# The order of TensorE's work in an attention stage, and who writes the rows of ones

## The chip, the core and the metric

The kernel runs on one core of a Trainium2 chip. The metric is the device time of one execution in microseconds (us), measured from outside; the profile's span is the part of it between the first and the last recorded instruction. Times below that come from the profile belong to one profiled execution. A core has five engines, each with its own queue of instructions: TensorE (PE, with its weight loads PEld), VectorE (DVE), ScalarE (ACT), GpSimd (POOL) and SyncE (SP), which here issues nearly all transfers (DMAs). An instruction that waits for a semaphore holds up all that is queued behind it on its engine.

## The reference, cut to what matters

The program is two transformer layers. The change touches the first attention alone: 2 sequences of 512 tokens, 32 query heads of width 8, of which each four share one of 8 key and value heads.

```python
q = bitlinear(x, wq).reshape(B, S, N_KV, G, HEAD_DIM)      # B 2, S 512, N_KV 8, G 4, HEAD_DIM 8
k = bitlinear(x, wk).reshape(B, S, N_KV, HEAD_DIM)
v = bitlinear(x, wv).reshape(B, S, N_KV, HEAD_DIM)
scores = jnp.einsum('bskgd,btkd->bkgst', q, k) * sm_scale
scores = jnp.where(causal, scores, -jnp.inf)
probs = jax.nn.softmax(scores, axis=-1)
out = jnp.einsum('bkgst,btkd->bskgd', probs, v)
```

Behind it come a gated feed-forward layer, a recurrent mixing layer with a scan over time, and a mixture of 32 experts with a shared one, each between layer norms with residuals. None of their instructions changes.

## The kernel before

The order of every engine's queue is written out by hand. The attention works on 16 groups (`NG`): one sequence and one key head with its four query heads, 512 by 512 scores a head. The scores of a group are computed twice. First as **rows** (queries on the partitions): VectorE takes from them the negated maximum of each query, `negm`. Then as **columns** (keys on the partitions): the maxima, brought back as extra rows of the query operand, are subtracted inside the product, so that ScalarE's exponential can write `probs` at once, keys first, as the product with the values wants them. The keys' operand `k_all` has rows of ones (partitions 32 to 63 and 96 to 127) which carry these extra rows through the product.

The loop is a software pipeline over slots n = 0 to 19 (`slots`). In slot n TensorE does, of group n, six units of score rows (`score_rows`, list `ROWS`); of group n-2, five pairs of score columns (`score_cols`, list `COLS`); of group n-3, the product with the values for four key tiles (`weighted`, called "value products" here); and in odd slots `out_rows`, which turns the finished outputs of two groups into rows. Before, the order within a slot is a loop over u = 0 to 5: rows u, then (u = 0, odd slot) `out_rows`, columns u, and value products by the table `PV_AT`.

What sets the order around it:
- Row units take turns on two pairs of PSUM banks: unit u waits until VectorE has reduced unit u-2 (`s1_read`). Columns take turns on three banks, two for a pair, so the next pair waits for ScalarE's first exponential of the pair before (`st_exp`).
- VectorE in slot n reduces the six row units. After unit 1 (`MT_AT`) it transposes the split maxima of group n-1 (`m_cols`), and in odd slots after unit 0 it divides (`DIV_AT`).
- ScalarE in slot n does the ten exponentials of group n-2, and in even slots after the last (`OC_AT` = 9) the copy `o_cols` for which the `out_rows` of the next slot waits.
- GpSimd zeroes the future keys in `probs` (four instructions a group, semaphore `hidden`) and between them splits the maxima of group n into two parts.
- SyncE in slot n loads the queries of group n+1 (`load_q`, six DMAs), then waits for `m_cols` of group n-1, writes it to DRAM in four DMAs (L545), waits for them, and loads it into the query operand in two (L549). The columns of group n-1 wait for these. In slot 1 it first loads the keys of the second sequence (`load_k(1)`, four DMAs) and their rows of ones (`ones_rows(1)`, two DMAs).

After the attention ScalarE and TensorE go on with the first output product and the feed-forward layer; what is behind it starts when the attention's last groups are done.

## Time and profile before

| | us |
|---|---|
| median of 3 runs (lowest, highest) | 647.87 (647.41, 648.37) |
| the profiled execution | 645.54 |
| its span | 643.8 |
| PE, DVE, ACT, POOL busy | 457.6, 385.6, 248.9, 231.4 |
| score rows of group 0 start on TensorE | 53.52 |
| first score columns start | 81.49 |
| one odd and one even slot in the steady part | 9.17 and 8.45 |

TensorE is busy for 71% of the span, but the mean hides stages with different limits: the profile's second section cuts the span in 40 slices of 16.1 us each, and the attention is slices 4 to 14. A busy TensorE is not one at full speed either; the row PEclk of that section gives the granted clock in tenths. The chain of waits is the view to read for what sets the end; the rows that are used stand below.

### The profile page before, as it was taken

What the parts mean: (1) busy time and instruction counts of PE and PEld (TensorE: products, weight loads), DVE (VectorE), ACT (ScalarE), POOL (GpSimd) and SP (SyncE); (2) the same over time, 40 slices, a digit from 0 to 9 for tenths busy, and PEclk for the clock granted to TensorE, in tenths of its full rate; (3) what the DMA queues carried; (4) which work ended last, traced back from release to release, by engine and by line L of the source; (5) the groups of instructions that cost most, each with busy time, mean ns of one, the idle gap of its engine ahead of it and who ended that gap; (6) DMA issues with size and microseconds to landing.
All of it is one profiled execution on the core that took longest, in us unless ns stands there. A gap on an engine that the chain in (4) does not pass through costs nothing.

```text
span 643.8 us, 9925 instructions
## 1 busy us (share of the span) xinstructions
PE 457.6 (71%) x3183; PEld 336.2 (52%) x3183; DVE 385.6 (60%) x940; ACT 248.9 (39%) x503; POOL 231.4 (36%) x310
## 2 busy tenths in 40 slices
PE   0365398888987869698954345596777999999660
PEld 0253254454444448577743334494665777877440
DVE  6833457777776256745497848863723555655344
ACT  1141056666668543225802450523312344433202
POOL 6911024333364631403102211165170455555500
PEclk9995559999999889897997566997897999999965
DMA  9177911111150039600000005984022344543061
GB/s 225 29 151 174 120 40 41 36 35 31 40 171 7 2 116 338 211 1 1 0 2 25 24 24 122 251 248 129 18 110 62 114 132 127 143 124 99 20 260 65
DMA packets 60146, 62.26 MB, mean 97 GB/s; under 512 B 10420, under 2 KB 51005, under 8 KB 60096
## 3 DMA queue, kind: packets, MB, share of 16 engines
q1 hardware_dynamic: 54928, 52.89, 32.4%
q0 software_dynamic: 5168, 8.74, 4.1%
q8 instruction: 27, 0.44, 0.3%
q14 instruction: 23, 0.19, 0.1%
HBM read 37.67 MB, written 25.75 MB: 99 GB/s over the span
## 4 chain that ended last, share of the span: by engine, by line
PE 49%; DVE 24%; issue 9%; ACT 6%; DMA 6%; POOL 2%; SPq 2%; another core or an unknown queue 1%; POOLq 0%; DVEq 0%; ACTq 0%
PE ps L2045 8%; PE ps L1789 5%; PE ps L2064 4%; PE ps L1839 4%; PE ps L1747 4%; PE ps L1768 4%; PE ps L1827 3%; PE ps L1828 3%; PE ps L1829 3%; PE ps L2035 3%; DVE xn L836 2%; DVE st L904 2%; DVE negm L1003 2%; DVE gain L1106 2%; ACT probs L1491 2%
## 5 line engine op out<-in xcount | busy, mean ns | idle before, releaser
L1491 ACT ACTIVATE probs<-ps 128x512 f32<-128x512 f32 x160 | 86.9, 595 | 66.6 <-PE ps L1768 64.8
L1000 DVE TENSOR_REDUCE negm<-ps 128x2 f32<-128x1024 f32 (+1 forms) x64 | 68.9, 1090 | 43.0 <-PE ps L1757 42.2
L813 POOL DMA_INDIRECT y_slots_scratch<-yblk,ids x63 | 62.0, 984 | 64.1 <-issue 26.4
L1747 PE MATMUL ps<-k_all,q_ring 64*128 64x512 f32 (+3 forms) x256 | 52.4, 416 | 22.6 <-DMA q_ring<-q_ring 10.8
L656 POOL TENSOR_TENSOR rstd<-ve,halfneg 128x4 f32<-128x4 f32 x16 | 16.6, 1035 | 128.6 <-DVE ve L935 80.6
L2045 PE MATMUL ps<-wgu,xcol 128*128 x252 | 58.1, 354 | 4.0 <-issue 1.5
L1768 PE MATMUL ps<-q_ring,k_all 64*128 64x512 f32 (+3 forms) x256 | 41.7, 382 | 19.1 <-DMA q_ring<-max_parts_scratch 9.9
L1747 PEld LDWEIGHTS ps<-k_all,q_ring 64*128 64x128 f32 x256 | 27.6, 207 | 48.5 <-issue 28.0
L1789 PE MATMUL ps<-probs,v_all 128*32 128x128 f32 (+3 forms) x512 | 47.0, 467 | 4.8 <-POOL probs L702 4.6
L2045 PEld LDWEIGHTS ps<-wgu,xcol 128*128 128x128 f32 x252 | 40.3, 193 | 12.6 <-issue 10.1
L1529 ACT CAST h_hi<-hf 128x512 fp32r<-128x512 f32 x28 | 17.4, 620 | 64.2 <-DVE hf L1058 55.6
L788 POOL DMA_INDIRECT x_sorted_scratch<-rows,dest x32 | 31.5, 984 | 25.9 <-DVE dest L1284 16.7
L1058 DVE TENSOR_TENSOR hf<-sg,ps 128x512 f32<-128x512 f32 x28 | 19.2, 685 | 35.9 <-ACT sg L1523 23.6
L702 POOL TENSOR_SCALAR_AFFINE_SELECT probs<-probs 128x512 f32<-128x512 f32 x64 | 39.8, 634 | 0.0
L2064 PE MATMUL ps<-wd,hcol 96*128 x126 | 38.7, 388 | 0.9 <-ACT yblk L1676 0.6
L1003 DVE TENSOR_REDUCE negm<-ps 128x4 f32<-128x1024 f32 (+1 forms) x32 | 29.3, 954 | 16.7 <-PE ps L1757 16.6
L1378 DVE TENSOR_TENSOR hb<-gb,ps 128x96 f32<-128x96 f32 x63 | 16.0, 253 | 35.3 <-ACT gb L1668 25.5
L1768 PEld LDWEIGHTS ps<-q_ring,k_all 64*128 64x128 f32 x256 | 22.0, 198 | 26.2 <-ACT probs L1491 14.1
L694 POOL TENSOR_TENSOR waited<-zero 128x1 f32<-128x1 f32 x48 | 9.2, 192 | 73.6 <-ACT probs L1491 73.5
L1361 DVE COPY xcol<-ps 128x256 f32<-128x256 f32 x63 | 26.6, 422 | 13.4 <-PE ps L2035 13.2
L1668 ACT ACTIVATE gb<-ps 128x96 f32<-128x96 f32 x63 | 15.8, 251 | 46.9 <-PE ps L2045 38.9
L1676 ACT COPY yblk<-ps 128x256 f32<-128x256 f32 x63 | 23.4, 372 | 24.0 <-PE ps L2064 22.4
(290 smaller groups left out, 1284.9 us busy)
## 6 DMA issues: line engine op xcount, KB each, us to landing
x_sorted_scratch<-pad SPq DMA_DIRECT2D x7, 1206.0 KB, 13.5
xblk<-x_sorted_scratch SPq DMA_DIRECT2D x63, 134.0 KB
wgu<-in_moe_w SPq DMA_DIRECT2D x4, 1536.0 KB
q_ring<-q_parts_scratch SPq DMA_DIRECT2D x64, 64.0 KB
ycomb<-y_slots_scratch SPq DMA_DIRECT2D x8, 512.0 KB, 6.9
wd<-in_moe_w SPq DMA_DIRECT2D x1, 3072.0 KB, 18.6
sraw<-in_moe_w SPq DMA_DIRECT2D x6, 384.0 KB, 3.3
k_all<-ones SPq DMA_DIRECT2D x4, 512.0 KB, 11.3
```

The costliest lines, as they stand in the source:

```text
L702: pool.affine_select(out=tiles, in_=tiles, compare_op=ALU.is_ge, fill=0.0, base=0, pattern=[[0, GQ], [1, P]], channel_multiplier=-1).then_ ...
L788: pool.indirect_dma_start(out=x_sorted, out_offset=bass.IndirectOffsetOnAxis(ap=dest[:, u, j:j + 1], axis=0), in_=rows[:, u, :], in_offset ...
L813: pool.indirect_dma_start(out=y_slots, out_offset=bass.IndirectOffsetOnAxis(ap=ids[:, i:i + 1], axis=0), in_=yblk[:, i % YR, :], in_offset ...
L1000: dve.tensor_reduce(negm[:, par, :, hp, qt], pair_of, AX.X, ALU.max, negate=True).then_inc(s1_read, 1)
L1003: dve.tensor_reduce(negm[:, par, :, :, qt], pair_of.rearrange("p a (h t) -> p a h t", h=nh), AX.X, ALU.max, negate=True).then_inc(s1_read, 1)
L1361: dve.tensor_copy(xcol[:, i % 2, :], ps[:, i % 2, 0:D]).then_inc(bt_copied, 1)
L1491: act.activation(probs[:, par, u, :], ps[:, col_unit(g, u), :], ACT.Exp)\
L1747: pe.matmul(ps[:, u % 2 * 2 + rg, end - w:end], q_ring[lane(rg, 64), g % QRING, h0 + h, qt * P:(qt + 1) * P], k_all[lane(rg, 64), g * T:g ...
L1768: mm = pe.matmul(ps[:, col_unit(g, 2 * p + rg), c:c + w], k_all[lane(rg, 64), g * T + kt * P:g * T + (kt + 1) * P], q_ring[lane(rg, 64), g ...
L1789: mm = pe.matmul(ps[32 * h:32 * h + 32, 7, kt * P:T], v_all[:, (g * TPB + kt) * 32:(g * TPB + kt + 1) * 32], probs[:, g % 2, un, c:c + T - ...
L2045: mm = pe.matmul(ps[:, 2 + i % 2, 0:2 * F].rearrange("p (w f) -> p w f", w=2), xcol[:, i % 2, k * P:(k + 1) * P], wgu[:, k, :, bass.ds(e * ...
L2064: pe.matmul(ps[:, 4 + i % 2, 0:D], hcol[0:F, i % 2, :], wd[0:F, bass.ds(e, 1), :].rearrange("p o d -> p (o d)"), start=True, stop=True).th ...
```

## The change

TensorE's order within a slot becomes a table, `ORDER`. `out_rows` stands at the head of an odd slot, then come the first pair of columns, and the last thing in a slot are the first two row units of the next group ("next"). The value products wait for as many of GpSimd's four instructions as they need (1, 2, 4, 4) and no longer all four. VectorE transposes the maxima after row unit 0. The product with the Hadamard matrix in slot 0 (L1873) moves from behind row unit 3 to behind row unit 4. The rows of ones are written by ScalarE, in four copies of 32 partitions by 4096 elements: two at its very start, one in slot 1 behind its last copy of slot 0, one in slot 2 behind the exponentials of group 0. SyncE's four DMAs for them go, and `load_k(1)` moves from slot 1 to the end of slot 3.

```diff
@@ -257,6 +257,7 @@
         s_x = [sem("x0_loaded"), sem("x1_loaded")]
         s_const = sem("consts_loaded")
         s_constb = sem("bf16_consts_loaded")
+        k_ones = sem("key_ones_rows_ready")
         s_w = sem("attn_weights_loaded")
         s_dve = sem("vector_order")
         s_pool = sem("pool_order")
@@ -396,8 +397,12 @@
         RU, CU, QD = len(ROWS), len(COLS), 96
         SLOTS = NG + 4
         FIRST, PAIRS = 4, 4
-        MT_AT, DIV_AT, OT_AT, OC_AT = 1, 0, 0, 9
-        PV_AT = {1: [0], 2: [1], 3: [2, 3]}
+        MT_AT, DIV_AT, OC_AT = 0, 0, 9
+
+
+        ORDER = (("cols", 0), ("rows", 2), ("values", 0), ("cols", 1), ("rows", 3), ("cols", 2),
+                 ("rows", 4), ("values", 1), ("rows", 5), ("cols", 3), ("values", 2),
+                 ("values", 3), ("next", 0), ("cols", 4), ("next", 1))
 
         def slots(body):
 
@@ -509,17 +514,6 @@
                         q_ring[64 * rg + MAX_AT + 2:64 * rg + MAX_AT + 4, g % QRING, :, :]
                         .bitcast(F32)).then_inc(q_in[g % 2], 16)
 
-            def ones_rows(b):
-
-                for rg in range(2):
-                    sp.dma_start(
-                        k_all[64 * rg + KP:64 * rg + 64, b * NKV * T:(b + 1) * NKV * T]
-                        .bitcast(F32).rearrange("r (n c) -> r n c", c=P),
-                        ones[0:64 - KP, :].unsqueeze(1).to_broadcast((64 - KP, NKV * T // P, P)))\
-                        .then_inc(k_in[b], 16)
-
-            sp.wait_ge(s_ready, 1)
-            ones_rows(0)
             spill(0)
             load_k(0)
             sp.wait_ge(q_spilled, 32)
@@ -530,9 +524,6 @@
             def slot(n, par, pair):
                 if n == 0:
                     spill(1)
-                if n == 1:
-                    load_k(1)
-                    ones_rows(1)
                 if n == FIRST - 1:
                     sp.wait_ge(q_spilled, 32 * B)
                 if 3 <= n + 1 < NG:
@@ -550,6 +541,8 @@
                             q_ring[64 * rg + MAX_AT:64 * rg + MAX_AT + 2, g % QRING, :, :]
                             .bitcast(F32), m_dram[g, rg].rearrange("(i hp) t -> i hp t", hp=2))\
                             .then_inc(m_in[g % 2], 16)
+                if n == 3:
+                    load_k(1)
 
 
                 after = n - (FIRST + 2 * PAIRS)
@@ -1428,6 +1421,16 @@
 
         @block.scalar
         def _(act):
+            def ones_rows(b, rg):
+
+                act.copy(k_all[64 * rg + KP:64 * rg + 64, b * NKV * T:(b + 1) * NKV * T]
+                         .rearrange("r (n c) -> r n c", c=P),
+                         ones[64 * rg + KP:64 * rg + 64, :].unsqueeze(1)
+                         .to_broadcast((64 - KP, NKV * T // P, P))).then_inc(k_ones, 1)
+
+            act.wait_ge(s_ready, 1)
+            ones_rows(0, 0)
+            ones_rows(0, 1)
             act.wait_ge(s_w, 64)
             for n in range(4):
                 cols = DC * (64 if n in (1, 2) else D)
@@ -1505,6 +1508,8 @@
                             1.0 / 32).then_inc(w2_hi_done, 1)
                     act.wait_ge(w2_hi_done, 1)
                     act.copy(w2hi[:, :, :], w2a[:, :, :]).then_inc(w2_hi_done, 1)
+                if n in (1, 2):
+                    ones_rows(1, n - 1)
                 if n in (NG - 2, NG - 1):
 
                     raw, hi = ((w1raw, w1hi), (w3raw, w3hi))[n - NG + 2]
@@ -1737,6 +1742,13 @@
             pe.wait_ge(k_split, B)
             pe.wait_ge(q_split, DC * B)
 
+            def rows_begin(g):
+
+                pe.wait_ge(q_in[g % 2], (g // 2 + 1) * QD)
+                if g % NKV == 0:
+                    pe.wait_ge(k_in[g // NKV], 64)
+                    pe.wait_ge(k_ones, 2 * (g // NKV + 1))
+
             def score_rows(g, u):
                 qt, h0, nh = ROWS[u]
                 need(pe, s1_read, RU * g + u - 1)
@@ -1783,7 +1795,7 @@
 
                 if kt == 0:
                     need(pe, att_ready, g // 2 * 2)
-                    pe.wait_ge(hidden, 4 * (g + 1))
+                pe.wait_ge(hidden, 4 * g + (1, 2, 4, 4)[kt])
                 for h in range(GQ):
                     un, c = WHERE[kt, h]
                     mm = pe.matmul(ps[32 * h:32 * h + 32, 7, kt * P:T],
@@ -1848,23 +1860,23 @@
                     pe.wait_ge(rows_ready, TPB)
                     transposes(1, 0, rows_tile(0))
                 if n == 0:
-                    pe.wait_ge(q_in[0], QD)
-                    pe.wait_ge(k_in[0], 96)
-                if has(n, 0) and n > 0:
-                    pe.wait_ge(q_in[par], pair * QD + QD)
-                if n == NKV:
-                    pe.wait_ge(k_in[1], 96)
-                for u in range(RU):
-                    if has(n, 0):
+                    rows_begin(0)
+                    score_rows(0, 0)
+                    score_rows(0, 1)
+                if has(n, 4) and n % 2:
+                    out_rows(n - 4)
+                for what, u in ORDER:
+                    if what == "rows" and has(n, 0):
                         score_rows(n, u)
-                    if u == OT_AT and has(n, 4) and n % 2:
-                        out_rows(n - 4)
-                    if has(n, 2) and u < CU:
+                    if what == "next" and has(n + 1, 0):
+                        if u == 0:
+                            rows_begin(n + 1)
+                        score_rows(n + 1, u)
+                    if what == "cols" and has(n, 2):
                         score_cols(n - 2, u)
-                    if has(n, 3) and u in PV_AT:
-                        for kt in PV_AT[u]:
-                            weighted(n - 3, kt)
-                    if n == 0 and u == 3:
+                    if what == "values" and has(n, 3):
+                        weighted(n - 3, u)
+                    if n == 0 and (what, u) == ("rows", 4):
 
                         pe.wait_ge(butterfly, 3)
                         pe.wait_ge(w2_split, 1)
@@ -1875,12 +1887,12 @@
                                     half[:, 2 * c:2 * c + 2, :].rearrange("p c d -> p (c d)"),
                                     start=(j == 0), stop=(j == 1))
                             mm.then_inc(w2_mm, 1)
-                    if n == NG and u == 2:
+                    if n == NG and (what, u) == ("values", 1):
 
                         pe.wait_ge(att_ready, NKV)
                         pe.wait_ge(s1_read, RU * NG)
                         transposes(0, 0, att_tile(0))
-                    if n == NG + 1 and u == 2:
+                    if n == NG + 1 and (what, u) == ("values", 1):
                         out_product(0)
 
             def mlp_up(u):
```

On TensorE, at the boundary between an even and an odd slot, this stands before (128x256 x4 are the last pair of columns, 128x128 x2 the last row unit, 128x512 x2 from `k_all` and `q_ring` the first row unit of the next group, `ident,o_cols` the turn `out_rows`, 128x512 x2 from `q_ring` and `k_all` the first pair of columns; the rows from `hide_cols` and `hide_swap` between them belong to the row units):

```order
L1768 MATMUL ps<-q_ring,k_all 128x256 x4
...
L1747 MATMUL ps<-k_all,q_ring 128x128 x2
...
L1747 MATMUL ps<-k_all,q_ring 128x512 x2
...
L1778 MATMUL ps<-ident,o_cols 128x128 x4
L1768 MATMUL ps<-q_ring,k_all 128x512 x2
```

And this at the same boundary after the change:

```order
L1780 MATMUL ps<-q_ring,k_all 128x128 x2
L1801 MATMUL ps<-probs,v_all 32x256 x4
L1801 MATMUL ps<-probs,v_all 32x128 x4
L1759 MATMUL ps<-k_all,q_ring 128x512 x2
...
L1780 MATMUL ps<-q_ring,k_all 128x256 x4
L1759 MATMUL ps<-k_all,q_ring 128x512 x2
...
L1790 MATMUL ps<-ident,o_cols 128x128 x4
L1780 MATMUL ps<-q_ring,k_all 128x512 x2
L1759 MATMUL ps<-k_all,q_ring 128x384 x2
```

Between the last pair of columns and `out_rows` there were two row units; now there is one.

On SyncE this stands before from the spill of the second sequence on (`k_parts_scratch`, `q_parts_scratch`) to the maxima of group 0:

```order
L477 DMA q_parts_scratch<-qparts_102 128x2x512
L485 DMA k_all<-k_parts_scratch 16x8x512 [waits k_parts_in_dram]
L485 DMA k_all<-k_parts_scratch 16x8x512 x3
L515 DMA k_all<-ones 32x32x128 x2
L545 DMA max_parts_scratch<-m_cols 32x32 [waits max_rows_ready]
L545 DMA max_parts_scratch<-m_cols 32x32 x3
L549 DMA q_ring<-max_parts_scratch 2x1024 [waits max_rows_even_in_dram]
```

And this after the change; the load of the keys stands 30 DMAs further on, behind the maxima of group 2:

```order
L482 DMA q_parts_scratch<-qparts_102 128x2x512
L536 DMA max_parts_scratch<-m_cols 32x32 [waits max_rows_ready]
L536 DMA max_parts_scratch<-m_cols 32x32 x3
L540 DMA q_ring<-max_parts_scratch 2x1024 [waits max_rows_even_in_dram]
L540 DMA q_ring<-max_parts_scratch 2x1024
```

Six DMAs in front of the first maxima are gone.

On ScalarE this is the start of the attention after the change; before, the two rows of `k_all` were not there:

```order
L1506 ACTIVATE w2a<-ps 128x2048 [waits w2_hadamard_done]
L1510 CAST w2hi<-w2a 128x2048 [waits w2_hi_ready]
L1426 CAST k_all<-ones 32x4096
L1494 ACTIVATE probs<-ps 128x512 [waits score_cols_full] x10
L1426 CAST k_all<-ones 32x4096
L1494 ACTIVATE probs<-ps 128x512 [waits score_cols_full] x10
```

The second of them stands between the exponentials of group 0 and those of group 1.

## Rows read from the trace of the kernel before

**Rows 1.** The page: the granted clock by slice of 16.1 us.
```profile
PEclk9995559999999889897997566997897999999965
```
**Rows 2.** The chain of waits in order of time: start us, us, what.
```profile
67.35 5.62 SPq L545
...
79.78 1.66 DMA q_ring<-max_parts_scratch
81.49 0.81 PE ps L1768 x2
```
**Rows 3.** SyncE's queue by time, 42 to 110 us: start, us, what.
```profile
61.73 2.54 SPq L485 DMA_DIRECT2D k_all<-k_parts_scratch  x4
64.31 1.33 SPq L515 DMA_DIRECT2D k_all<-ones  x2
...
102.47 1.80 SPq L545 DMA_DIRECT2D max_parts_scratch<-m_cols  x4
105.32 0.52 SPq L549 DMA_DIRECT2D q_ring<-max_parts_scratch  x2
```
**Rows 4.** DMA issues, 60 to 200 us: KB each, median us to landing.
```profile
k_all<-k_parts_scratch SPq DMA_DIRECT2D x4, 256.0 KB, 7.9
k_all<-ones SPq DMA_DIRECT2D x2, 512.0 KB, 12.8
...
max_parts_scratch<-m_cols SPq DMA_DIRECT2D x56, 4.0 KB, 1.4
```
**Rows 5.** VectorE by time, around slots 0 to 2.
```profile
62.83 1.82 DVE L1003 TENSOR_REDUCE negm<-ps 128x4 f32<-128x1024 f32 x2 [4.01 <-PE ps L1757]
...
69.58 1.82 DVE L1003 TENSOR_REDUCE negm<-ps 128x4 f32<-128x1024 f32 x2 [0.45 <-PE ps L1757]
```
**Rows 6.** ScalarE by time, start of the program and slots 0 to 3.
```profile
10.62 1.55 ACT L1434 ACTIVATE wsg<-wraw 128x512 fp32r<-128x512 f32 x4 [8.55 <-DMA wraw<-in_wo]
...
63.48 1.90 ACT L1507 CAST w2hi<-w2a 128x2048 fp32r<-128x2048 f32 x1
82.33 1.09 ACT L1491 ACTIVATE probs<-ps 128x512 f32<-128x512 f32 x2 [16.95 <-PE ps L1768]
```
**Rows 7.** Windows: stretch, length, busy of PE, PEld, DVE, ACT, POOL, then granted clock.
```profile
66.00:68.00 2.00, 1.48 (x12) 0.82 (x12) 2.00 (x4) 0.00 (x0) 0.00 (x0) 0.58 1.13 130
82.00:92.00 10.00, 9.49 (x74) 6.13 (x70) 6.86 (x8) 6.51 (x12) 3.31 (x9) 0.50 0.18 47
94.00:96.00 2.00, 2.00 (x26) 1.05 (x28) 0.96 (x1) 1.08 (x2) 0.33 (x1) 1.00 0.06 10
143.33:152.50 9.17, 8.06 (x100) 4.51 (x101) 6.96 (x11) 5.90 (x12) 3.30 (x9) 1.00 0.13 36
152.50:160.95 8.45, 7.35 (x96) 4.10 (x97) 6.22 (x8) 5.43 (x12) 3.30 (x9) 1.00 0.14 36
```
**Rows 8.** TensorE by time in the steady part: slot from 152.5 us, head of the next.
```profile
154.17 0.50 PE L1768 MATMUL ps<-q_ring,k_all 64*128 64x512 f32 x2 [0.41 <-ACT probs L1491]
...
155.59 0.45 PE L1747 MATMUL ps<-k_all,q_ring 64*128 64x384 f32 x2
...
159.37 0.49 PE L1768 MATMUL ps<-q_ring,k_all 64*128 64x256 f32 x4
...
160.95 0.51 PE L1747 MATMUL ps<-k_all,q_ring 64*128 64x512 f32 x2 [0.69 <-DVE negm L1003]
...
161.51 0.66 PE L1778 MATMUL ps<-ident,o_cols 128*128 128x128 f32 x4
162.10 0.51 PE L1768 MATMUL ps<-q_ring,k_all 64*128 64x512 f32 x2
```
**Rows 9.** ScalarE by time behind the last pair of columns of that slot.
```profile
159.90 1.09 ACT L1491 ACTIVATE probs<-ps 128x512 f32<-128x512 f32 x2 [0.73 <-PE ps L1768]
160.87 0.59 ACT L1499 COPY o_cols<-ps 128x512 f32<-128x512 f32 x1
```
**Rows 10.** VectorE by time: the division behind that `out_rows`.
```profile
163.19 0.49 DVE L1028 TENSOR_TENSOR att<-ps,rsum 128x128 f32<-128x128 f32 x2
```

## The prediction, on record before the run

> **What bounds the kernel now.** I read the clock row of the page first, then the chain of waits in order of time, then each engine's own timeline in the stretch that the change touches. The clock row [rows 1] is to be read as stages: slices 4 to 6 (48 to 96 us) stand at 5, half speed, the rest of the attention at 9 or full. So the attention has two parts, and the change means something else in each.
>
> The head, 53.5 to 94 us. The chain [rows 2] runs through transfers: the write of group 0's maxima to DRAM is issued at 67.35, one of its four issues takes 5.62 us, and only at 81.49 do the first score columns start. In SyncE's queue [rows 3] the reader is to see what stands in front: the keys of the second sequence at 61.73 and their rows of ones at 64.31. These are 4 x 256 KB and 2 x 512 KB, 2 MB, and take 7.9 and 12.8 us to land, where the maxima (4 KB each) take 1.4 us in the median [rows 4]. Later the same six DMAs of a group need 105.32 - 102.47 = 2.85 us from the first issue to the load back [rows 3]; the load itself lands in about 1.7 us [rows 2]. In the head it was 81.49 - 67.35 = 14.1 us in place of some 4.5.
>
> The steady part, 94 to 206 us. A pair of slots takes 9.17 + 8.45 = 17.62 us, at full clock, TensorE busy 8.06 and 7.35 of it [rows 7]. Its timeline shows two waits in the even slot [rows 8]: 0.69 us for VectorE's maxima ahead of row unit 0 and 0.41 us for an exponential ahead of the second pair of columns. Measured on the queue, from the end of issue and not from the modelled end of the matmuls, I take them as 0.85 and 0.5. Twice, that is 2.7 us a pair, and leaves 14.9 us of TensorE's own work.
>
> **The head after the change.** Six DMAs go from in front of the maxima, so the round trip is 4.5 us. It also starts earlier: the Hadamard product (3.7 us, during which VectorE idled 4.01 us [rows 5]) now has row unit 4 in front of it, whose reduction (1.24 us) is thereby hidden, and the transpose comes one reduction (1.14 us) sooner. 67.35 - 1.2 - 1.1 is about 65.5 for the issue, 70.3 for the maxima back in place. Now VectorE is late next: group 1's reductions, which ended at 71.40 [rows 5], end at about 70.5 to 71, and TensorE reaches the first columns behind the second row unit of group 2, at about 72.1. The head gains 81.5 - 72.1 = **9.4 us**. If the spill of the second sequence, still in flight, holds the maxima up by half of what they lost before, 4.7 us of this go.
>
> **The rows of ones on ScalarE.** A copy of 2048 elements took 1.90 us [rows 6], so one of 4096 is 3.8 us at most. The Trainium skill ("ScalarE: Activation LUTs", What ACT_TABLE_LOAD costs) gives 0.833 ns an element plus 186 ns, thus 3.60 us; by that each copy is 0.2 us cheaper, and the 2048 of the row, 1.89 us, agree. Two copies fill 2.1 to 9.7 us, where ScalarE idled until 10.62 [rows 6]: nothing. The third follows the copy that ends at 65.4, before an idle time of 16.95 us [rows 6]: nothing. The fourth has no such cover: it stands between the exponentials of groups 0 and 1. The gap there is small, and TensorE has one row unit and the first value products (about 1.7 us at half clock) to do before it needs the exponential. 3.8 - 1.7 - 0.2 leaves **+1.9 us**, bounds 0 and 3.8. `load_k(1)` at the end of slot 3 costs SyncE 2.54 us of issue [rows 3], is needed in slot 7, and can make group 3's maxima late by about a microsecond; they have about that slack: 0, up to +1.
>
> **The steady part.** The exchange of order is costed wait by wait, from the timelines.
> - Row unit 0 no longer waits at the head of a slot: two row units are issued ahead and VectorE's queue is full. -0.85 twice a pair. VectorE's own work (6.96 and 6.22 us [rows 7]) is less than TensorE's, so it takes the place only where its queue is held up (below).
> - `out_rows` waits for `o_cols`. From the start of the last pair of columns (159.37 [rows 8]) ScalarE starts its two exponentials at 159.90 and the copy at 160.87, which lasts 0.59 [rows 9]; `out_rows` began at 161.51, 2.14 us after the columns, and there the chain fits to a hair: row unit 5, the wait for VectorE and row unit 0 lay over it. Now only one row unit is in between. Columns 0.32 and row unit 0.46 are 0.78 us, so TensorE waits 2.14 - 0.78 = **1.36 us** in each odd slot. This wait did not exist before.
> - The value products behind it wait for the division. `out_rows` lasts 0.6 [rows 8]; the division is a reciprocal and two products, 0.87 us, and with hand-overs the value products may start 1.75 us after `out_rows`; columns 0 and row unit 2 fill 1.3: +0.45 in the odd slot. Before, the division ended at 163.68 [rows 10], just ahead of the value products.
> - The second pair of columns has row unit 2 and value products in front, together 1.4 us (second pair and value products last from 154.17 to 155.59 [rows 8], the pair 0.43 of it, row unit 2 0.38): its 0.5 us goes, twice. But the third follows the second after one row unit: 0.43 + 0.38 = 0.81 us, where the exponential that it waits for is ready some 1.2 us after the start of its columns (0.53 to its start, half of 1.09 for itself, and up to 0.1 more for the wider columns and the hand-over [rows 8, 9]). +0.4 in the odd slot, +0.3 in the even one, where other waits cover a part.
> - In the even slot the first pair of columns follows the last pair of the slot before after 0.78 us: +0.4.
> - GpSimd splits the maxima behind its zeroing, and the fourth pair of columns now comes behind row unit 5. So the split comes some 2 us later than before, and VectorE's transpose, behind reduction 0, waits for it and holds up reduction 1 by 0.6 us. Row units 2 and 3 then wait 0.2 us together in the even slot; in the odd slot the wait for `out_rows` covers it.
>
> New waits 1.36 + 0.45 + 0.7 + 0.4 + 0.2 = 3.1 us, old ones 2.7: 14.9 + 3.1 = **18.0 us a pair**, against 17.62. Six pairs (slots 4 to 15) are **+2.4 us**. The bounds: no wait at all gives 14.9 and -16.3 us; all of them with 0.25 us more for each hand-over (8 a pair) give 20.0 and +14.
>
> **The sum.** -9.4 + 1.9 + 2.4 = -5.1. The end of the attention has no row units to interleave and the same chain over GpSimd: 0, I take +0.2. The profiled execution took 645.54 and would take 640.6. The median of the runs is 2.3 us above that execution; the same -4.9 puts it at **643.0 us**. All that stands behind the attention waits for its last groups, so it moves along.
>
> The half clock of the head is taken along unchanged: it rose between 92 and 96 us, some 12 us after dense work began at 81.5 [rows 7]. If it rises as long after 72.1, at 84 us, nothing changes in the sum; if only where it did before, TensorE has one slot more at half speed, +2 us. The Trainium skill ("TensorE: Matmul & The Clock Gate", Part 1) says that the same kernel can leave the low clock at different points from run to run; it would widen this to either side and sets no term.
>
> **The rivals.**
> - *The waits vanish.* The order was laid out so that each wait finds work in front of it. If TensorE ran without waits from slot 4 on, 643.0 - 2.4 - 16.3 is 624; half of that, 634. For it: no engine but TensorE is over 80% busy in [rows 7]. Against: `out_rows` has 0.78 us of cover for a chain of 2.14 us that rows 8 and 9 show link by link.
> - *The clock falls in the new waits* (slower). At 66 to 68 us TensorE was busy 1.48 of 2 us and was granted 0.58 [rows 7]. The odd slots get a gap of 1.36 us with more to follow. A slot at half clock needs about 12 us for what takes 8, so +4; from two such slots on the head's gain is gone, four give 643 + 16 = 659. Against: before, gaps of 0.85 us and a busy share of 87% kept the full clock, and it will be 83%.
> - *The head does not gain.* The maxima of group 0 land behind the spill anyway, at 77 to 81 us. Then 643.0 + 4.7 to 9 is 648 to 652. Against: the spill is 1.5 MB and the queue accepted the loads behind it at once at 61.73 [rows 3].
>
> **How the numbers follow.** The forecast has 0.74, its own range 639 to 647. The waits that vanish, wholly or by half, have 0.12, the clock 0.07, the head without gain 0.07. Range 634 to 648. Within 0.2% (1.3 us), about what a measurement of this kernel tells from no change, is 646.6 to 649.2. Faster: 0.12 and 0.67 of the forecast's 0.74, 0.79. Same: 0.06 of the forecast and 0.04 of the last rival, 0.10. Slower: 0.01 and 0.03 of these and the clock's 0.07, 0.11.
>
> **What would show it.** The first columns at about 72 us and no long wait for `max_parts_scratch`. An idle ScalarE replaced by a 3.8 us copy before group 1, with TensorE waiting behind it. In the steady part: no wait of row unit 0 for VectorE; `out_rows` waiting for `o_cols`, 1.4 us in every second slot; the third pair of columns waiting for an exponential; pairs of 18.0 us. Pairs well under 17.6 us, or first columns later than 76 us, would make it wrong.

## The result, and the profile after

The changed kernel took 649.99 us in the median of 19 runs (646.61 to 656.07), the kernel before 646.02 us (638.54 to 648.69, 19 runs): ratio 1.0088, 95% interval 1.0059 to 1.0118. The forecast was 643.0 us, 634 to 648. The kernel is slower by 4 us, and the prediction is wrong in sign. A second set, of 12 runs beside 29 of the kernel before, gave 1.0052 (1.0012 to 1.0092). The ratios leave out the executions that took over 1.5% longer than the fastest one of the same kernel; where that is more than one, the text says so.

The profiled execution of the changed kernel is the longest of its 19: 656.07 us, span 654.3. That of before took 645.54, span 643.8. So the two traces are 10.5 us apart where the medians are 4.0 apart, and each stage below has to be read with a second profile of the changed kernel (650.24 us) beside it.

The page's clock row, which answers to [rows 1], shows where to look: the seventh slice (98 to 115 us) stands at 6 where before it was 9, the 13th and 14th (196 to 229 us) at 7 and 6 where they were 9 and 8. The sixth is better, 8 against 5.

```profile
PEclk9985686999997688998996576988787999999966
```

I cut both traces at the same landmarks: the starts of the first columns of groups 0, 2, 4, 14 and 15, the first matmul of the output product and the first one of the MLP (the feed-forward layer). For the changed kernel the six stages, and one steady pair of slots between them, are, in windows (stretch, length, busy of PE, PEld, DVE, ACT, POOL with the number of instructions, then granted clock, DMA share, GB/s):

```profile
71.30:92.40 21.10, 18.51 (x165) 10.86 (x161) 12.85 (x15) 14.09 (x21) 5.24 (x14) 0.64 0.36 59
92.40:114.90 22.50, 19.68 (x196) 10.57 (x196) 13.43 (x18) 11.31 (x22) 7.12 (x21) 0.77 0.29 44
122.04:130.46 8.42, 6.41 (x82) 3.49 (x80) 6.60 (x10) 4.82 (x9) 3.05 (x8) 1.00 0.14 38
130.46:140.06 9.60, 8.77 (x124) 5.10 (x124) 6.64 (x8) 6.51 (x12) 3.49 (x11) 1.00 0.12 34
114.90:207.00 92.10, 77.94 (x970) 43.37 (x970) 65.41 (x85) 58.54 (x107) 36.42 (x90) 0.96 0.19 55
207.00:219.60 12.60, 9.07 (x62) 4.56 (x62) 0.37 (x2) 8.57 (x15) 9.45 (x15) 0.73 0.02 3
219.60:227.09 7.49, 5.56 (x25) 1.42 (x25) 1.89 (x5) 3.56 (x7) 4.33 (x2) 0.50 0.01 2
227.09:246.28 19.19, 12.05 (x96) 9.12 (x93) 9.84 (x34) 4.39 (x8) 4.86 (x9) 0.77 0.19 57
```

The kernel before, same stages:

```profile
81.50:99.60 18.10, 16.89 (x158) 10.09 (x160) 11.32 (x13) 10.85 (x20) 5.45 (x14) 0.67 0.14 36
99.60:117.20 17.60, 15.38 (x200) 8.59 (x200) 13.17 (x18) 11.33 (x21) 6.61 (x18) 1.00 0.14 38
117.20:205.50 88.30, 76.76 (x980) 42.84 (x979) 65.25 (x85) 58.01 (x106) 37.66 (x92) 1.00 0.20 57
205.50:217.40 11.90, 8.06 (x62) 4.16 (x62) 1.13 (x4) 8.61 (x15) 8.83 (x14) 0.86 0.02 3
217.40:221.59 4.19, 3.17 (x25) 0.95 (x24) 1.90 (x5) 3.15 (x7) 4.19 (x2) 1.00 0.02 4
221.59:237.89 16.30, 10.47 (x97) 6.83 (x93) 9.85 (x34) 4.80 (x10) 5.14 (x10) 0.90 0.22 66
```

Length and clock have to be read together. The changed kernel reaches the first columns at 71.3 in place of 81.5 us and is slower in every stage behind them: +3.0, +4.9, +3.8, +0.7, +3.3 and +2.9, and another 2.1 in all that follows, from the first MLP matmul to the end. Less 10.2 that is the 10.5. Wherever it loses more than a microsecond, its granted clock is below before's.

The same stages of all kernels that ran; in brackets the granted clock of the long steady stage (five pairs of slots). "Out" is the output product, "0 to 2" the us from the first columns of group 0 to those of group 2:

| kernel | first columns | 0 to 2 | 2 to 4 | 4 to 14 | 14 to 15 | 15 to out | out to MLP | ratio to before, 95% |
|---|---|---|---|---|---|---|---|---|
| before | 81.5 | 18.1 | 17.6 | 88.3 (1.00) | 11.9 | 4.2 | 16.3 | |
| changed | 71.3 | 21.1 | 22.5 | 92.1 (0.96) | 12.6 | 7.5 | 19.2 | 1.0088 (1.0059 to 1.0118) |
| changed, again | 73.0 | 22.7 | 17.9 | 95.1 (0.93) | 11.6 | 7.6 | 19.0 | 1.0052 (1.0012 to 1.0092) |
| head alone | 72.1 | 23.6 | 17.6 | 87.9 (1.00) | 12.9 | 5.7 | 17.0 | 0.9919 (0.9891 to 0.9946) |
| order alone | 83.0 | 18.3 | 18.1 | 90.9 (0.98) | 11.6 | 7.5 | 19.2 | 1.0228 (1.0187 to 1.0268) |
| copy after exp 7 | 71.0 | 22.6 | 17.1 | 85.8 (1.00) | 8.9 | 8.0 | 19.0 | 0.9912 (0.9886 to 0.9939) |
| wait filled | 72.7 | 22.7 | 18.0 | 89.7 (1.00) | 11.6 | 7.1 | 19.0 | 0.9979 (0.9943 to 1.0015) |
| old end | 72.5 | 22.7 | 18.0 | 95.0 (0.93) | 13.1 | 4.2 | 16.3 | 1.0024 (0.9985 to 1.0062) |
| last values late | 71.3 | 22.6 | 18.0 | 95.1 (0.93) | 10.0 | 7.2 | 17.3 | 1.0033 (1.0006 to 1.0059) |
| copies in slot 1 | 72.0 | 19.9 | 25.1 | 95.1 (0.93) | 12.0 | 7.2 | 19.0 | 1.0120 (1.0087 to 1.0152) |
| dense order | 72.7 | 19.4 | 19.3 | 83.3 (1.00) | 8.9 | 6.6 | 16.9 | 0.9898 (0.9867 to 0.9929) |
| copy 7, values late | 71.2 | 21.1 | 17.7 | 85.7 (1.00) | 8.9 | 7.3 | 18.2 | 0.9932 (0.9901 to 0.9962) |
| old order, free copies | 72.5 | 17.8 | 22.8 | 87.9 (1.00) | 13.7 | 6.1 | 16.8 | 0.9935 (0.9907 to 0.9963) |
| all together | 72.0 | 17.2 | 16.8 | 83.3 (1.00) | 8.9 | 7.0 | 17.0 | 0.9671 (0.9610 to 0.9731) |

**The head** did what it was to do. In SyncE's queue of the changed kernel the load of the maxima is issued 68.29 - 65.55 = 2.7 us behind their first write, where it was 79.78 - 67.35 = 12.4 us in [rows 2]. From that first write to the first columns it is 71.30 - 65.55 = 5.8 us, against 14.1:

```profile
65.55 1.73 SPq L536 DMA_DIRECT2D max_parts_scratch<-m_cols  x4
68.29 0.52 SPq L540 DMA_DIRECT2D q_ring<-max_parts_scratch  x2
```

ScalarE shows the price. The third copy lies in idle time. The fourth starts at 80.26, behind the exponentials of group 0, and those of group 1 that are ready meanwhile follow at 83.88 in a block of six:

```profile
66.81 3.60 ACT L1426 CAST k_all<-ones 32x4096 fp32r<-32x4096 f32 x1
...
80.26 3.60 ACT L1426 CAST k_all<-ones 32x4096 fp32r<-32x4096 f32 x1
83.88 3.46 ACT L1494 ACTIVATE probs<-ps 128x512 f32<-128x512 f32 x6
```

**The steady part.** Where the clock is full it is as forecast: 8.42 + 9.60 = 18.02 us a pair, against 17.62 in [rows 7]. TensorE's waits, 100 to 205 us (us in total, times, longest):

```profile
PE ps L1790 <- ACT o_cols L1502: 8.0, 6, 1.3
PE ps L1780 <- ACT probs L1494: 6.0, 16, 0.5
PE ps L1801 <- DVE att L1021: 1.3, 5, 0.3
```

TensorE by time at the head of an odd slot, which answers to [rows 8]:

```profile
157.82 0.48 PE L1780 MATMUL ps<-q_ring,k_all 64*128 64x256 f32 x4
...
159.96 0.66 PE L1790 MATMUL ps<-ident,o_cols 128*128 128x128 f32 x4 [1.33 <-ACT o_cols L1502]
```

`out_rows` begins 159.96 - 157.82 = 2.14 us behind the last pair of columns, to the hundredth the same chain as before, and now the engine stands still for 1.33 us of it. What the forecast did not have is the windows around that wait:

```profile
140.00:142.00 2.00, 0.67 (x11) 0.37 (x10) 1.44 (x2) 1.56 (x3) 1.92 (x7) 1.00 0.20 53
158.00:160.00 2.00, 0.67 (x11) 0.37 (x9) 1.44 (x2) 1.56 (x3) 1.92 (x7) 1.00 0.21 63
160.00:162.00 2.00, 1.74 (x16) 0.99 (x20) 1.31 (x4) 0.85 (x2) 0.45 (x1) 0.90 0.30 85
162.00:164.00 2.00, 2.00 (x10) 0.50 (x4) 1.53 (x2) 0.24 (x1) 0.00 (x0) 0.50 0.06 8
```

Behind the wait at 158 the granted clock falls to half (1.2 GHz) and TensorE, busy throughout, does less. Behind the equal one at 140 it does not.

**The end of attention.** TensorE by time from slot 17 on, in the changed kernel:

```profile
218.97 0.66 PE L1790 MATMUL ps<-ident,o_cols 128*128 128x128 f32 x4 [1.66 <-ACT o_cols L1502]
219.56 0.78 PE L1780 MATMUL ps<-q_ring,k_all 64*128 64x512 f32 x2
221.57 1.93 PE L1801 MATMUL ps<-probs,v_all 128*32 128x512 f32 x8 [1.24 <-DVE att L1021]
223.44 0.79 PE L1780 MATMUL ps<-q_ring,k_all 64*128 64x512 f32 x2
224.93 0.80 PE L1780 MATMUL ps<-q_ring,k_all 64*128 64x384 f32 x4 [0.69 <-ACT probs L1494]
...
234.61 1.71 PE L1801 MATMUL ps<-probs,v_all 128*32 128x512 f32 x16 [2.48 <-POOL probs L695]
236.59 0.86 PE L1801 MATMUL ps<-probs,v_all 128*32 128x256 f32 x16 [0.27 <-POOL probs L695]
240.87 1.97 PE L1813 MATMUL ps<-ident,rows 128*128 128x128 f32 x8 [3.43 <-DVE rows L971]
```

and before:

```profile
216.78 0.66 PE L1778 MATMUL ps<-ident,o_cols 128*128 128x128 f32 x4 [1.66 <-ACT o_cols L1499]
217.37 0.50 PE L1768 MATMUL ps<-q_ring,k_all 64*128 64x512 f32 x2
218.62 0.50 PE L1768 MATMUL ps<-q_ring,k_all 64*128 64x512 f32 x2 [0.75 <-ACT probs L1491]
219.38 1.07 PE L1789 MATMUL ps<-probs,v_all 128*32 128x512 f32 x8 [0.27 <-DVE att L1028]
...
229.94 4.05 PE L1789 MATMUL ps<-probs,v_all 128*32 128x512 f32 x32 [4.56 <-POOL probs L702]
234.14 1.09 PE L1801 MATMUL ps<-ident,rows 128*128 128x128 f32 x8
```

Two edits show here. The value products stand ahead of the second columns and wait 1.24 us for the division, which the second columns used to cover. And the last group's value products no longer wait for all four zeroings; they run early in two pieces, and TensorE then idles 3.43 us ahead of the transposes, which take 1.97 us in place of 1.09, half clock.

The wait of 1.66 us ahead of `out_rows` is in both kernels. Behind it the changed kernel's first columns already run at half clock (0.78 us at 219.56), those of before at full clock (0.50 us at 217.37). The same fall is found once with the old order: in *old order, free copies* the waits of this stage are before's, and it takes 6.05 us at clock 0.53 in place of 4.19 at 1.00:

```profile
213.69 1.12 PE L1779 MATMUL ps<-ident,o_cols 128*128 128x128 f32 x4 [1.66 <-ACT o_cols L1498]
```

So not all of the 3.3 us need be the order's. From group 15's columns to the MLP the six profiles with the changed kernel's end have 26.1 to 27.1 us, the four with the old one (before, head alone, old end, old order with free copies) 20.5 to 22.8: the order costs 3.3 to 6.6 us there, and the 6.2 of these two traces stand near the upper end.

### The profile page after: what moved, and what is told of

Read it like the earlier page. It is cut to its first block, busy times and chain, and to the rows that moved or that the text cites. A ratio compares the mean times of both kernels' runs of the same rounds, so it can differ in the third digit from the quotient of the medians.

```text
span 654.3 us, 9927 instructions
## 1 busy us (share of the span) xinstructions
PE 471.6 (72%) x3183; PEld 344.6 (53%) x3183; DVE 385.7 (59%) x940; ACT 263.4 (40%) x507; POOL 231.0 (35%) x310
## 4 chain that ended last, share of the span: by engine, by line
PE 48%; DVE 23%; issue 10%; ACT 8%; DMA 4%; POOL 2%; SPq 1%; another core or an unknown queue 1%; POOLq 0%; DVEq 0%; ACTq 0%
PE ps L2057 7%; PE ps L1801 5%; PE ps L1780 5%; PE ps L2076 4%; PE ps L1851 4%; PE ps L1759 4%; ACT probs L1494 3%; PE ps L2047 3%; PE ps L1839 2%; PE ps L1841 2%; DVE st L897 2%; PE ps L1840 2%; DVE xn L829 2%; DVE gain L1099 2%; PE ps L1813 2%
## 5 line engine op out<-in xcount | busy, mean ns | idle before, releaser
L993 DVE TENSOR_REDUCE negm<-ps 128x2 f32<-128x1024 f32 (+1 forms) x64 | 67.0, 1080 | 33.9 <-PE ps L1769 33.0
L1801 PE MATMUL ps<-probs,v_all 128*32 128x128 f32 (+3 forms) x512 | 51.5, 502 | 5.3 <-POOL probs L695 2.7
L1780 PE MATMUL ps<-q_ring,k_all 64*128 64x512 f32 (+3 forms) x256 | 45.2, 412 | 12.8 <-ACT probs L1494 12.3
L1534 ACT CAST h_hi<-hf 128x512 fp32r<-128x512 f32 x28 | 17.3, 619 | 66.9 <-DVE hf L1051 56.9
L1780 PEld LDWEIGHTS ps<-q_ring,k_all 64*128 64x128 f32 x256 | 23.9, 215 | 36.0 <-ACT probs L1494 25.7
L1051 DVE TENSOR_TENSOR hf<-sg,ps 128x512 f32<-128x512 f32 x28 | 19.2, 684 | 37.1 <-ACT sg L1528 20.8
L1371 DVE TENSOR_TENSOR hb<-gb,ps 128x96 f32<-128x96 f32 x63 | 15.9, 253 | 34.7 <-ACT gb L1673 20.5
## 6 DMA issues: line engine op xcount, KB each, us to landing
wd<-in_moe_w SPq DMA_DIRECT2D x1, 3072.0 KB, 19.1
```

What stands on the lines that cost most here:

```text
L993: dve.tensor_reduce(negm[:, par, :, hp, qt], pair_of, AX.X, ALU.max, negate=True).then_inc(s1_read, 1)
L1780: mm = pe.matmul(ps[:, col_unit(g, 2 * p + rg), c:c + w], k_all[lane(rg, 64), g * T + kt * P:g * T + (kt + 1) * P], q_ring[lane(rg, 64), g ...
L1801: mm = pe.matmul(ps[32 * h:32 * h + 32, 7, kt * P:T], v_all[:, (g * TPB + kt) * 32:(g * TPB + kt + 1) * 32], probs[:, g % 2, un, c:c + T - ...
```

## The experiments

Four kernels ran together on each of three chips; the kernel before took 648.39 us on the first, 630.56 on the second, 644.26 on the third (medians of 17, 22 and 29 runs). Kernels of different chips are compared by their ratios and by their stages up to the MLP.

**Head alone.** The kernel before with the rows of ones by ScalarE and `load_k(1)` in slot 3.

```
-            sp.wait_ge(s_ready, 1)
-            ones_rows(0)
...
-                if n == 1:
-                    load_k(1)
-                    ones_rows(1)
+                if n == 3:
+                    load_k(1)
...
+                if n in (1, 2):
+                    ones_rows(1, n - 1)
```

> The kernel before with only the rows of ones written by ScalarE and load_k(1) moved behind slot 3; TensorE's order stays the old one. Theory A (the head gains what was forecast, and the loss comes from the new order): first score columns at about 71 to 73 us in place of 81.5, then a stall of up to 2 us behind the fourth copy, median 7 to 9 us below the kernel before, near 638. Theory B (the head's gain is given back later, hidden by something downstream): first columns early all the same, but the median within 2 us of the kernel before.

643.05 us in the median of 6 (639.71 to 644.66). Of the 9.4 us at the first columns 3.9 are left at group 2's: stage 0 to 2 takes 23.6 us in place of 18.1. So in the old order too the fourth copy and the half clock behind it take 5.5 us. The median is 5.3 us below before's, between what the two theories said (7 to 9, and within 2).

**Order alone.** The new order, the waits and the new places of transpose and split, with the old transfers.

```
-                    pe.wait_ge(hidden, 4 * (g + 1))
+                pe.wait_ge(hidden, 4 * g + (1, 2, 4, 4)[kt])
...
+                for what, u in ORDER:
```

> The changed kernel's order of TensorE's work, but rows of ones by DMA and load_k(1) in slot 1 as before. Theory A: first score columns near 80 us again and the slower steady part, so 7 to 9 us above the changed kernel, 656 to 660, some 11 us above the kernel before. Theory B: about as the changed kernel, 650.

661.86 us (658.23 to 667.32, 6 runs), above theory A's 656 to 660. The order is what makes the kernel slower, by 1.0228 (1.0187 to 1.0268), far more than the 2.4 + 0.2 of the prediction. Against before, the first columns are 1.5 us later, and the stages +0.2, +0.5, +2.6, -0.3, +3.3 and +2.9: 6.2 of 10.7 us lie in the last two, which the sum had at 0.2. The profiled run is the shortest of its six, 3.6 us under their median.

**Copy after exp 7.** The changed kernel with the copy of the output columns two exponentials earlier on ScalarE.

```
-        MT_AT, DIV_AT, OC_AT = 0, 0, 9
+        MT_AT, DIV_AT, OC_AT = 0, 0, 7
```

> The changed kernel with one number other: ScalarE copies o_cols behind the eighth exponential and not behind the tenth (OC_AT 7), so out_rows at the head of the odd slot finds it ready. Theory A1 (the wait of out_rows, 1.33 us in each odd slot, makes the steady part slow, and it also lets TensorE's clock fall): pairs of 16.7 us at full clock in place of 18.0, no half clock between 95 and 200 us, 12 to 16 us below the changed kernel, near 636. Theory A2 (the wait costs its own length and the clock falls anyhow, by other waits or by chance): pairs of 16.7 us where the clock is full, but stretches of half clock as before, 8 us below the changed kernel, near 642.

642.71 us (642.08 to 644.04, 6 runs). The wait for `o_cols` is gone and one for the division is there, 100 to 200 us:

```profile
PE ps L1780 <- ACT probs L1494: 8.5, 18, 1.2
PE ps L1801 <- DVE att L1021: 3.4, 5, 0.9
```

The stage of five pairs takes 85.8 us, 17.2 a pair, at clock 1.00, and group 14 to 15 takes 8.9 us in place of 12. One number moved by two gives back 1.8% of the kernel against the changed one's first ratio, 1.4% against its second. The clock is as theory A1 said; the pair is 17.2 and not 16.7 us, because the waits for the exponentials (8.5 us in place of 6.0) and the division have grown. The edit takes away wait and falls of the clock together; the next run parts them.

**Wait filled.** The changed kernel, the row unit ahead of `out_rows` issued three times over, so that the wait has work in it but the chain is as long.

```
-                for h in range(nh):
+                for h in [h for _ in range(times) for h in range(nh)]:
...
-                        score_rows(n + 1, u)
+                        score_rows(n + 1, u, 3 if u == 1 and n % 2 == 0 and has(n + 1, 4) else 1)
```

> The changed kernel with the wait ahead of out_rows filled: in front of each out_rows the matmuls of the row unit ahead are issued three times over, with the same result, which adds 0.9 us of work where TensorE waited 1.33. The order and every other wait stay. Theory A1 (the gap in TensorE's work is what drops its clock): pairs stay at 18.0 us, but no half clock between 95 and 200 us, 5 to 8 us below the changed kernel, near 643. Theory A2 (the clock falls by chance, and alike in both kernels): no gain, 650, or up to 1 us slower by the work added.

650.85 us in the median of 12, spread from 641.7 to 653.5; ratio 0.9979. That ratio is of the seven shortest runs; the medians of all give 1.0038. So the stage below is shown, a gain in the whole time is not clear of the noise, and theory A1's 643 was not reached. In windows the steady stage:

```profile
113.40:203.10 89.70, 79.34 (x1030) 45.29 (x1030) 65.27 (x85) 58.44 (x107) 36.90 (x93) 1.00 0.20 57
```

More instructions, the same chain, 17.9 us a pair and full clock throughout. The changed kernel again, in its second profile:

```profile
113.60:208.70 95.10, 81.02 (x968) 44.84 (x969) 65.49 (x85) 58.49 (x107) 36.97 (x93) 0.93 0.17 54
```

5.4 us is what the clock takes there, comparing two profiles of two kernels. The cost of the wait itself, the 18.0 us pair, is in both.

**Old end.** The changed kernel with the old order of second columns and first value products from slot 16 on, and the old wait for groups 13 to 15.

```
-                pe.wait_ge(hidden, 4 * g + (1, 2, 4, 4)[kt])
+                pe.wait_ge(hidden, 4 * g + (4 if g >= NG - 3 else (1, 2, 4, 4)[kt]))
...
+                if n >= NG:
+                    order = tuple(ORDER[i] for i in (0, 1, 3, 2) + tuple(range(4, len(ORDER))))
```

> The changed kernel, with the old order at the end of attention alone: from slot 16 on the second columns stand ahead of the first value products again, and the value products of the last three groups wait for all four zeroings again. Slots 0 to 15 are the new ones. Theory A (the new order costs some 7 us in the last slots and 2 us at the start of the MLP, because the chain columns, exponential, zeroing, value products, division has nothing beside it there, and because TensorE pauses ahead of the last transposes): from the first columns of group 14 to the first MLP matmul 33 to 34 us in place of 39.3, the MLP up to 2 us shorter, ratio to the kernel before 1.0088 - 0.010 = 0.995 to 1.000. Rival B (the end is long only because TensorE's clock is low there, whatever the order of the last slots): that stretch stays at 37 to 39 us, ratio 1.005 to 1.010. Rival C (what slots 14 and 15 leave over, rows issued early, is late and not the slots behind): the stretch from group 14's to group 15's columns stays over 12 us and the rest is as before the change, 35 to 36 us in all, ratio 1.000 to 1.004.

634.04 us (626.01 to 636.84, 11 runs), ratio 1.0024 of the eight shortest (the medians of all give 1.0055). The end, in windows:

```profile
221.30:225.49 4.19, 3.17 (x26) 0.95 (x25) 1.89 (x5) 3.16 (x7) 4.19 (x2) 1.00 0.02 4
225.49:241.77 16.28, 10.45 (x97) 6.82 (x93) 9.84 (x34) 4.80 (x10) 5.16 (x10) 0.90 0.20 66
```

Both stages are before's to the hundredth, clock included, and 33.6 us from group 14's columns to the MLP in place of 39.3 and 38.2. Theory A is right on these stages. The stage ahead of them stays at 13.1 us, as rival C said, at clock 0.74. The ratio is above theory A's 0.995 to 1.000 and in rival C's 1.000 to 1.004, with an interval that reaches to 1.0062, into that of the changed kernel: the steady stage has the clock at 0.93 here too. The gain is shown in the stages, not in the whole time.

**Last values late.** Of the two edits at the end, the wait alone, for group 15 alone.

```
-                pe.wait_ge(hidden, 4 * g + (1, 2, 4, 4)[kt])
+                pe.wait_ge(hidden, 4 * g + (4 if g == NG - 1 else (1, 2, 4, 4)[kt]))
```

> The changed kernel, the value products of the last group (15) alone waiting for all four zeroings ahead of the first of them, as before the change, so that they stand close in front of the transposes of the attention's last rows. Theory A (TensorE's pause of 3.4 us between these value products and the transposes is what lets the clock fall, at which the transposes and the first 10 us of the MLP then run): the transposes at full clock, the stretch from group 14's columns to the first MLP matmul about 1 to 2 us shorter than 39.3, the MLP 2 us shorter, ratio 0.3 to 0.6% under the changed kernel's 1.0088, about 1.004. Rival B (the pause moves ahead of the value products and they run at half clock themselves, four times longer in the chain): no gain or a loss of up to 1 us, ratio 1.008 to 1.011. No other stretch should change but by the falls of the clock that differ from run to run.

633.2 us (628.39 to 635.7, 12 runs), ratio 1.0033, near theory A's 1.004, but its interval overlaps that of the changed kernel's second set. TensorE by time, and a window over the start of the value products:

```profile
233.49 3.87 PE L1801 MATMUL ps<-probs,v_all 128*32 128x512 f32 x32 [4.56 <-POOL probs L695]
237.69 1.09 PE L1813 MATMUL ps<-ident,rows 128*128 128x128 f32 x8 [0.33 <-DVE rows L971]
```

```profile
233.00:235.00 2.00, 1.51 (x8) 0.46 (x12) 1.84 (x9) 0.00 (x0) 0.35 (x2) 0.54 0.19 65
```

A longer wait, 4.56 us, and then dense work straight into the transposes, which take 1.09 us, full clock. The clock fell all the same: the value products start at 0.54, as rival B said, and it is back at 1.00 before the transposes. That costs nothing, because the transposes start 9.24 to 9.26 us behind the last columns in this kernel, in the changed one and in before: the rows that they turn are not ready earlier. From the output product to the MLP it is 17.3 in place of 19.1 us; the transposes and what follows them are 1.7 of it (3.74 us from their start to the MLP, against 5.41). The other 1.0 of that stage is the output product at the half clock that it finds (224.16 to 227.21, 3.05 us, against 2.07 before). It and 15 to out come back only in *old end*, which undoes the exchange of columns and value products too.

**Copies in slot 1.** The changed kernel with the fourth copy beside the third.

```
-                if n in (1, 2):
-                    ones_rows(1, n - 1)
+                if n == 1:
+                    ones_rows(1, 0)
+                    ones_rows(1, 1)
```

> The changed kernel with both late copies of the ones rows on ScalarE in slot 1, where ScalarE idles, and none in slot 2. Theory A (the fourth copy, 3.60 us ahead of the exponentials of group 1, holds TensorE up by what it is not covered): the wait ahead of the value products of group 0 in slot 3 shrinks, group 2's first columns at 90 to 91 us in place of 92.4, ratio 0.2 to 0.4% under the changed kernel's 1.0088, so 1.005 to 1.007. Rival B (ScalarE is then late with its part of group 0, which takes the gain back: the two copies last 7.2 us from about 65): first columns of group 0 as before at 71.3 but its exponentials begin after 73, no gain, ratio 1.008 to 1.010.

637.55 us (635.99 to 642.96, 6 runs), ratio 1.012: slower than both theories said. The stage 0 to 2 gained, 19.9 in place of 21.1 to 22.7, but 2 to 4 took 25.1 at clock 0.73, behind a wait of TensorE for queries of 2.7 us. The next but one shows where that is from.

**Dense order.** Both copies in slot 1, the copy of the output columns after exponential 7, and more value products in between.

```
-        MT_AT, DIV_AT, OC_AT = 0, 0, 9
+        MT_AT, DIV_AT, OC_AT = 0, 0, 7
...
+        ORDER = (("cols", 0), ("rows", 2), ("values", 0), ("cols", 1), ("rows", 3),
+                 ("values", 1), ("cols", 2), ("rows", 4), ("values", 2), ("cols", 3),
+                 ("rows", 5), ("values", 3), ("cols", 4), ("next", 0), ("next", 1))
```

> The changed kernel with both late copies in slot 1, the copy of the output columns behind the eighth exponential in place of the tenth (as in the run that did this alone, pairs 17.2 us) and another order in a slot: columns 0, rows 2, values 0, columns 1, rows 3, values 1, columns 2, rows 4, values 2, columns 3, rows 5, values 3, columns 4 and the two row units of the next group. Theory A (what is left of waits in the steady part is the chain from one pair of columns to the next but one with a single row unit between, and each value product in between covers it): pairs of slots 16.0 to 16.6 us, slots 2 to 14 under 100 us, no wait of over 0.3 us for an exponential, ratio 0.980 to 0.988 (633 to 639 us against 646). Rival B (the value products issued so early wait for GpSimd's zeroings and the division, and the waits only change their name): pairs 17.2 us or more, ratio 0.990 or more. Rival C (the last slots are worse still): pairs shorter, but over 38 us from group 14's columns to the MLP, ratio 0.987 to 0.992.

623.45 us (621.22 to 626.67, 6 runs), ratio 0.9898. The pairs are 83.3 / 5 = 16.7 us, a little over what theory A said, and the wait for an exponential, 90 to 210 us, is 2.3 us in all, in three waits of up to 1.2. The ratio misses theory A's range by 0.2%. The 19.3 us for groups 2 to 4 are part of that, with the same wait for queries (1.7 us). Rival B is true in a small part: in the steady stage TensorE now waits 3.0 us for the division and 2.2 us for VectorE's maxima. Rival C is out: the end is 32.4 us.

**Old order, free copies.** The head alone, both late copies ahead of ScalarE's wait for the Hadamard product.

```
+                if n == 0:
+
+                    ones_rows(1, 0)
+                    ones_rows(1, 1)
                     act.wait_ge(w2_mm, HC // 2)
```

> The kernel before with the change's head alone, and both late copies of the ones rows put in slot 0 ahead of ScalarE's wait for the Hadamard product, where it idled 17 us. Theory A (of the head's gain of 9.4 us at the first columns the fourth copy, 3.60 us in front of group 1's exponentials, took 5.5 by group 2): first columns at 72 us, group 2's at 90 to 91 us, no wait of TensorE over 1.5 us in slots 2 and 3, ratio 0.985 to 0.989. Rival B (the half clock of the head takes it, which ends no sooner than after so much dense work): group 2's columns at 93 to 95 us, ratio 0.990 to 0.993. Rival C (two copies of 7.2 us hold up the Hadamard product's reading): first columns at 74 us or later.

641.09 us (637.08 to 642.72, 12 runs), ratio 0.9935. Theory A's stages came, its ratio (0.985 to 0.989) did not: 0 to 2 is 17.8 us, so the copies are free there, and group 2's columns start at 90.3. Then 2 to 4 takes 22.8. SyncE's queue and TensorE's waits by time:

```profile
87.10 2.52 SPq L486 DMA_DIRECT2D k_all<-k_parts_scratch  x4
...
93.35 1.88 SPq L532 DMA_DIRECT2D max_parts_scratch<-m_cols  x4
101.13 0.52 SPq L536 DMA_DIRECT2D q_ring<-max_parts_scratch  x2
```

```profile
100.34 0.50 PE L1748 MATMUL ps<-k_all,q_ring 64*128 64x512 f32 x2 [2.74 <-DMA q_ring<-q_ring]
...
102.93 0.80 PE L1769 MATMUL ps<-q_ring,k_all 64*128 64x512 f32 x2 [0.97 <-DMA q_ring<-max_parts_scratch]
```

101.13 - 93.35 = 7.8 us for 4 x 4 KB that take 2.85 in [rows 3], behind 1 MB of keys whose pieces land after 7.5 us. It is the old trouble of the head, moved to slot 4. The rule that fits is in the Trainium skill ("DMA: Bandwidth & Descriptors", HWDGE ordering): a completion's semaphore write lands only after every earlier write of that transfer engine. This trace agrees, but small writes that merely queue behind the same bytes would look alike, and no run here tells the two apart. The changed kernel has it in a milder form, since its group 2 comes later: 99.74 - 94.89 = 4.9 us in the same place of its first profile, a wait of 0.5 us, and 17.9 us for groups 2 to 4 in its second.

**Copy 7, values late.** The two one-line edits together.

```
-        MT_AT, DIV_AT, OC_AT = 0, 0, 9
+        MT_AT, DIV_AT, OC_AT = 0, 0, 7
...
+                pe.wait_ge(hidden, 4 * g + (4 if g == NG - 1 else (1, 2, 4, 4)[kt]))
```

> The changed kernel with two edits that were each run alone: the copy of the output columns behind the eighth exponential in place of the tenth, and the value products of the last group waiting for all four zeroings. Theory A (the two costs are independent: 1.76% and 0.55% by the ratios of the two runs to the changed kernel's 1.0088): steady pairs 17.2 us, no half clock in slots 4 to 15, 34 us from group 14's columns to the MLP, 3.4 us at half clock at its start, ratio 0.984 to 0.988. Rival B (both runs gained by the same thing, fewer falls of the clock): no more than the better of the two, 0.990 to 0.994.

639.55 us (634.86 to 643.11, 12 runs), ratio 0.9932 (0.9901 to 0.9962), no better than the earlier copy alone at 0.9912 (0.9886 to 0.9939). The stages came nearly as in theory A (85.7 at clock 1.00; 18.2 from out to MLP in place of 19.0), the ratio as in rival B. The profiled run is the shortest of its 12, so its stages flatter it. That the gains add isn't shown.

**The changed kernel again.** No edit; a second profile.

> The changed kernel unaltered, a second profile of it and its ratio beside the kernels of this call. Theory A (the slow end and the slow start of the MLP belong to the order, the falls of the clock in slots 4 to 15 to chance): 39 us again from group 14's first columns to the MLP and half clock in the MLP's first 10 us, but another number of falls between 100 and 210 us (after the profile of the changed kernel had three of them), ratio 1.005 to 1.012. Rival B (the falls sit at fixed places): falls at 103, 162 and 199 us again, give or take a microsecond. Rival C (the end is chance too): 33 to 35 us to the MLP.

649.57 us (641.85 to 654.97, 12 runs). The slow end comes again: 38.2 us from group 14 to the MLP. The slow start of the MLP doesn't: its first 10 us have clock 1.00 here and 0.80 in the first profile, against theory A. The falls of the clock in the steady part are at other places (142 to 146 and 180 to 190 us), and *old end* has its own within a microsecond of these. So the places are not fixed; what rule they follow, if any, these runs do not show.

**All together.** Dense order, copies in slot 0, the last values late, and the keys spread.

```
-                if n == 3:
-                    load_k(1)
+                if 3 <= n < 7:
+                    load_k(1, (((n - 3) // 2, (n - 3) % 2),))
```

> The dense order (values 1 and 2 each ahead of the next columns, both row units of the next group last, copy of the output columns behind the eighth exponential), both late copies of the ones in slot 0, the last group's value products waiting for all four zeroings, and the load of the second sequence's keys spread as one DMA each over slots 3 to 6. Theory A (the dense order alone had 0.9898 although its pairs are 16.6 us, because 11.6 us went by between the columns of groups 3 and 4: maxima and queries landed 4.5 us late behind the 1 MB of keys, and the clock fell in that wait): first columns at 72, group 2's at 90 to 91, then 8.3 us a slot throughout, group 14's columns at about 191, no half clock between 95 and 200 us, ratio 0.972 to 0.980. Rival B (the head's half clock lasts longer in kernel time when dense work starts sooner): group 2's columns at 93, ratio 0.980 to 0.985. Rival C (the keys arrive late for slot 7 now, a wait of over 1 us for them there): ratio 0.982 or more.

628.39 us (620.42 to 630.88, 6 runs) beside 644.26: ratio 0.9671 (0.9610 to 0.9731), better than both kernels. That ratio is of the four shortest runs; the medians of all give 0.9754, within theory A's 0.972 to 0.980, and the longest run is below the shortest of the kernel before (639.69). First stages, in windows:

```profile
72.00:89.20 17.20, 17.08 (x165) 10.11 (x160) 12.19 (x15) 10.48 (x20) 4.84 (x14) 0.66 0.19 44
89.20:106.00 16.80, 15.58 (x196) 8.47 (x196) 13.37 (x18) 11.34 (x22) 6.65 (x19) 1.00 0.29 56
```

In the head TensorE is busy 17.08 of 17.20 us, and it has the full clock from group 2 to group 15. Three edits part this kernel from *dense order*, and none of them was added alone. By the stages 0 to 2 is 2.2 us shorter, where the copies are, and 2 to 4 is 2.5 us shorter, where the keys are.

## Why the prediction was wrong

**First columns, -9.4:** right. 71.3 and 73.0 against 72.1 forecast, -10.2 and -8.5, and TensorE reached the columns without a wait for the maxima. One step has a slip that luck covered: 67.35 - 1.2 - 1.1 is 65.05 and not 65.5, and the write was issued at 65.55. The rival without gain in the head (0.07) is out.

**The fourth copy, +1.9, bounds 0 to 3.8:** the stall is right, what stands behind it is not. The copy lasts 3.60 us, the figure drawn from the Trainium skill ("ScalarE: Activation LUTs", What ACT_TABLE_LOAD costs), not the 3.8 of the rows. Stage 0 to 2 costs +3.0 and +4.6 in the two profiles of the changed kernel and +5.5 in the old order, and -0.3 there when the copies are in idle time. Of these, TensorE's idle time is +1.4, +1.5 and +2.3, about the 1.9 forecast. The rest, +1.6, +3.1 and +3.2, is longer busy time at a lower clock. The step that failed in the head is "the half clock of the head is taken along unchanged": in the old order the stage has clock 0.54 with the copy and 0.68 without it. In the changed kernel's first profile the clock was 1.00 at 84 to 86 us and back at 0.62 and 0.52 from 86 to 90, behind the stall.

**The steady pair, 18.0:** right, 18.02, with the waits near what was computed: 1.33 for `o_cols` against 1.36, about 6.0 / 6 = 1.0 a pair for the exponentials against 1.1, at most 0.3 for the division against 0.45. As 0.4 us a pair this is the +2.4 of the sum. Full-clock stages of the new order are 89.7 us long (wait filled) against 88.3.

**The clock falls in the new waits (0.07, 659 us):** this rival is true and was set too low. All six profiles with the bare wait of 1.33 us have a clock under 1.00 in the steady stage (0.93 to 0.98) and take 1.2 to 5.4 us more than the 89.7 of the filled one. The eight without it (old order; wait filled; copy after exp 7; dense) have 1.00. I argued from the average, 83% busy against 87%, which hides the wait: around it TensorE is busy 0.67 of 2 us. That row alone doesn't decide either, since it is the same at 140 us, where the clock stayed. The rival's price was four slots of 4 us, 16 us; the falls cost 1.2 to 5.4 us in the steady stage, a third of a slot to not quite one and a half. In the first profile another fall, at 103 us, goes with 22.5 us for groups 2 to 4, against 17.9 in the second.

**The end of attention, "0, I take +0.2":** this is the step that turned the sign. It cost +3.3 from group 15 to the output product and +2.9 from there to the MLP, 6.2 us in one profile and 6.1 in the other. I wrote that this stretch has "the same chain over GpSimd". It has the same chain but not the same cover: the second columns stood over the division before, and the new order puts them behind it. Of the 3.3, the waits are 1.24 + 0.69 against 0.75 + 0.27, so 0.9; the other 2.4 is TensorE's busy time, 5.56 against 3.17 us, for the same instructions at clock 0.50 against 1.00. The 2.9 are all clock: 1.25 the output product at half clock, 1.7 the last transposes and what follows them, behind the pause of 3.43 us, and these 1.7 are given back by one wait made later. So the term left out 0.9 us of waits and some 5.3 us of half clock. Of the clock's part, up to 2.3 us is found with the old end too (22.8 us from group 15 to the MLP against 20.5), so the order's own cost is 3.3 to 6.6 us.

**The sum.** -4.9 forecast. Up to the MLP the two profiles of the changed kernel are 8.4 and 9.0 us later than before's, while the medians differ by 4.0 and 5.3. What is behind, from the first MLP matmul to the end, makes up a part of the difference, and varies by itself: the same instructions took 405.9 us before and 408.0 and 401.6 in the two profiles of the changed kernel, and on one chip 401.0 at clock 0.88 in one kernel and 408.1 at 0.86 in another (head alone, copy after exp 7). What decides between these is open.

## What to carry to other kernels

Cost a reordering in every stretch where it runs, above all where the work that fills the gaps has run out: this order costs 0.4 us in a full pair of slots, and 3.3 to 6.6 in the last ones. A new wait has two prices, its own length and what the clock does behind it; a busy share over a whole stage hides the second. If the chain can't be shortened, look for an idle engine's earlier slot or a single position in its queue (here, one copy two places earlier). A bulk transfer taken away from in front of small ones can stand in front of other small ones where it is put (here 1 MB of keys, 7.8 us in place of 2.85); in pieces of 256 KB a slot it went with the shortest stage of all kernels here.

## What the runs showed of the hardware

- The granted clock fell behind a pause of 1.33 us with TensorE busy 0.67 of 2 us, but not behind each: at 140 us it stayed, at 158 us it fell. With work put into the pause it was 1.00 for 89.7 us. A pause of 1.66 us, the same in all, left the clock at 1.00 in before and in *old end*, and had half clock behind it in the changed kernel and in *old order, free copies*.
- A pause of 4.56 us had the matmuls behind it start at clock 0.54; after 4 us of them the transposes were at full clock (1.09 us). A pause of 3.43 us directly ahead of the same transposes had them at half (1.97 us).
- The kernel before took 630.56, 644.26, 646.02 and 648.39 us in four sets of 17 to 29 runs, three of them on known and different chips, a spread of 2.8% where kernels were to be told apart by 1%.
